# Matmuls of ones between the statistics matmuls ahead of the first loop

## What is computed

```python
xn = _layernorm(x, axis=-1)
# attention: one head of width 512
qkv = einsum('bsc,cf->bsf', xn, Wqkv) + bqkv
q, k, v = qkv.reshape(B, S, 3, 512)[:, :, 0], [:, :, 1], [:, :, 2]
attn = softmax(einsum('bqd,bkd->bqk', q, k) / sqrt(512))
attn_out = einsum('bqd,dc->bqc', einsum('bqk,bkd->bqd', attn, v), Wo) + bo
# 64 experts of rank 8, 16 of them chosen for each token
scores = einsum('bsr,er->bse', einsum('bsd,rd->bsr', xn, Wq_w), keys)
gate = softmax of the 16 largest scores at their places, 0 elsewhere
z = einsum('bsd,nd->bsn', xn, A_w) * gate (8 columns for each expert)
ffn_out = einsum('bsn,on->bso', z, B_w) * 2
out = x + attn_out + ffn_out
```

## Time and profile before

| | before |
|---|---|
| median of 3 runs | 2691.65 us (2690.94 to 2693.8) |
| the profiled execution | 2693.37 us |
| its span | 2691.5 us |
| TensorE matmul busy | 2645.6 us, 98% |
| TensorE weight loads busy | 2166.9 us, 81% |
| VectorE busy | 1884.6 us, 70% |
| ScalarE busy | 980.0 us, 36% |
| GpSimd busy | 346.1 us, 13% |
| DMA | 648.30 MB, mean 241 GB/s |

### The profile page before, as it was taken

One profiled execution on the slowest core, in us unless ns is written; L12 is line 12 of the kernel. 1 busy time (PEld: TensorE's weight loads), 2 busy tenths in 40 slices (PEclk: granted clock), 3 DMA queues, 4 the chain that ended last, 5 costly groups with the idle time before them and its releaser, 6 DMA issues.

```text
span 2691.5 us, 32557 instructions
## 1 busy us (share of the span) xinstructions
PE 2645.6 (98%) x11728; PEld 2166.9 (81%) x11728; DVE 1884.6 (70%) x2423; ACT 980.0 (36%) x1297; POOL 346.1 (13%) x334
## 2 busy tenths in 40 slices
PE   6999999999999999999999999999999999999998
PEld 5777887888878888888888888888888888888787
DVE  7958875567755777676847486684976838668677
ACT  5562335522364234433335332234332333223311
POOL 1011000000000001111103221022220212103140
PEclk9999999999999999999999999999999999999999
DMA  8689856445554457766887758578687775856866
GB/s 321 208 321 343 267 175 196 156 166 183 176 201 139 169 180 242 247 207 233 296 291 290 265 203 301 203 259 314 237 291 273 257 286 204 303 204 244 312 247 222
DMA packets 250915, 648.30 MB, mean 241 GB/s; under 512 B 20864, under 2 KB 45568, under 8 KB 246528
## 3 DMA queue, kind: packets, MB, share of 16 engines
q1 hardware_dynamic: 200528, 471.02, 50.2%
q0 software_dynamic: 30224, 111.16, 11.5%
q10 hardware_dynamic: 20000, 63.99, 6.6%
HBM read 499.27 MB, written 146.83 MB: 240 GB/s over the span
## 4 chain that ended last, share of the span: by engine, by line
PE 82%; DVE 6%; DMA 6%; issue 3%; ACT 3%; SPq 0%; ACTq 0%; DVEq 0%; POOL 0%
PE psum L843 38%; PE psum L2019 13%; PE psum L2021 13%; PE psum L2020 13%; PE psum L773 2%; DMA w_raw<-W_blocks 2%; DMA r_lo<-split_scratch 1%; DMA part_out<-v_scratch 1%; DVE part_out L2430 1%; ACT rows L621 1%; DMA part_out<-x 1%; ACT w_hi L548 1%; DVE r_lo L2303 0%; DVE w_lo L904 0%; DMA xb<-x 0%
## 5 line engine op out<-in xcount | busy, mean ns | idle before, releaser
L904 DVE TENSOR_TENSOR w_lo<-w_raw,w_hi 128x1024 fp32r<-128x1024 f32 x216 | 264.3, 1224 | 353.0 <-ACT w_hi L548 353.0
L548 ACT ACTIVATE w_hi<-w_raw 128x1024 fp32r<-128x1024 f32 x216 | 229.2, 1061 | 676.0 <-PE psum L843 620.8
L843 PE MATMUL psum<-s_hi,w_hi 128*128 128x512 f32 x896 | 352.4, 393 | 8.7 <-DVE rq L1120 3.1
L843 PE MATMUL psum<-w_hi,s_hi 128*128 128x512 f32 x896 | 349.6, 390 | 2.8 <-DVE w_lo L904 2.0
L843 PE MATMUL psum<-s_hi,w_lo 128*128 128x512 f32 x896 | 350.6, 391 | 0.0
L843 PE MATMUL psum<-s_lo,w_hi 128*128 128x512 f32 x896 | 350.6, 391 | 0.0
L843 PE MATMUL psum<-w_hi,s_lo 128*128 128x512 f32 x896 | 348.9, 389 | 0.0
L843 PE MATMUL psum<-w_lo,s_hi 128*128 128x512 f32 x896 | 348.8, 389 | 0.0
L843 PEld LDWEIGHTS psum<-s_hi,w_hi 128*128 128x128 f32 x896 | 169.2, 189 | 48.5 <-issue 8.2
L2019 PE MATMUL psum<-p_hi,r_hi 128*128 128x512 f32 x512 | 203.7, 398 | 3.9 <-DMA r_lo<-split_scratch 2.3
L843 PEld LDWEIGHTS psum<-w_hi,s_hi 128*128 128x128 f32 x896 | 168.2, 188 | 42.0 <-issue 3.8
(11 more groups left out here) (210 smaller groups left out, 4846.6 us busy)
## 6 DMA issues: line engine op xcount, KB each, us to landing
r_hi<-split_scratch SPq DMA_DIRECT2D x208, 512.0 KB, 3.5
r_lo<-split_scratch SPq DMA_DIRECT2D x208, 512.0 KB, 4.6
w_raw<-t_scratch SPq DMA_DIRECT2D x120, 512.0 KB, 4.1
w_raw<-W_blocks SPq DMA_DIRECT2D x104, 512.0 KB, 4.2
split_scratch<-rows POOLq DMA_DIRECT2D x56, 512.0 KB, 4.2
part_out<-x POOLq DMA_DIRECT2D x28, 1024.0 KB, 12.9
out<-part_out SPq DMA_DIRECT2D x28, 1024.0 KB, 8.4
rows<-x ACTq DMA_DIRECT2D x26, 1024.0 KB, 5.5
```

The costliest lines, as they stand in the source:

```text
L548: nc.scalar.activation(w_hi[:, s % RAW], w_tile(g, idx, s), ACT.Copy).then_inc(s_whi, 1)
L843: mm = pe.matmul(psum[:, bank, :], stationary, moving, start=(k == 0 and n == 0 and not chained), stop=(k == HK - 1 and n == 2), skip_grou ...
L904: nc.vector.tensor_tensor(w_lo[:, s % RAW], w_tile(g, idx, s), w_hi[:, s % RAW].bitcast(F32), ALU.subtract).then_inc(s_wlo, 1)
```

## The change

In the tensor program, `idle_matmuls(n)` is new: n matmuls of `ones` by `ones` into the columns 0 to 127 of bank 5, with no wait and no semaphore. It is called with 9 after the mean of tile j = 1 has been spread and ahead of the wait for tile j = 2, with 3 after the last of the four means (the increment of `s_spread` hangs on the matmul before them), and with 6 after the four reciprocal deviations, ahead of the loop. Other engines' programs are as before.

```diff
@@ -872,13 +872,21 @@
                                    part[:, 2, HT + a, j * P:(j + 1) * P], start=True, stop=True)
                 mm.then_inc(s_spread, 1)
 
+        def idle_matmuls(n):
+
+            for _ in range(n):
+                pe.matmul(psum[:, 5, 0:P], ones[:], ones[:], start=True, stop=True)
+
         pe.wait_ge(s_ones, 2)
         for a in range(2):
             for j in range(HT):
+                if a == 0 and j == 2:
+                    idle_matmuls(9)
                 pe.wait_ge(s_diag, HT + 1 if a else j + 1)
                 mm = pe.matmul(psum[:, 6 + a, j * P:(j + 1) * P], ones[:], stat_diag[a][:, j, :],
                                start=True, stop=True)
             mm.then_inc(s_spread, 1)
+            idle_matmuls((3, 6)[a])
         loop(pe, body)
```

## The result

The changed kernel takes 2696.2 us (median of 20 runs, 2692.52 to 2702.26), the kernel before 2691.99 us (20 runs beside it, 2688.04 to 2696.31). The ratio is 1.0014, with a 95% interval of 1.0008 to 1.0020: 4.2 us slower. I had forecast 2691.2 us and a range up to 2694.3.

A forecast was written before the change was run, and what follows sets the result against it. TensorE was taken to bound the kernel, carrying 82% of the chain. Free batches and a faster clock put it 2.9 us ahead, of which 0.5 passes: 2691.65 - 0.5 = 2691.2 us, range 2688.0 to 2694.3.

The forecast's parts named there:

- the cost of the batches: TensorE's head: batches of 9, 3 and 6 take 3.84, 1.28 and 2.56 us within idle time; cost zero, bounds -0.5 to +0.15.
- the clock: First products from 25.09 us: the matmuls of ones bring full pace, 3.2 instead of 6.11 us, TensorE 2.9 us ahead.
- Rival B: Head of TensorE: products of ones don't lift the clock, so nothing changes; 2691.65 us, chance 0.18.
- Rival D: Head batches: matmuls rewriting the same 128 columns don't stream, 0.58 us per record; 2700.0 us, chance 0.03.
- the 0.5 us at the end of the three points: Head: third weight tile, ScalarE's statistics and VectorE are late next, so 0.5 of the 2.9 us gained leaves the head.
- It removes nothing and moves nothing: Whole kernel: the change only adds 18 matmuls, 36 records, with no wait and no semaphore.
- Point 1: Third weight tile in the head: its load takes 13.2 us, so the item starts at 39.1; 1.7 of 2.9 us left.
- C: Later waits: early TensorE makes one idle stretch long enough for the clock to fall, costing 1.6 us; 2692.8 us, chance 0.06.

The follow-up runs named there:

- e3: The changed kernel without the batch of 9; the batches of 3 and 6 stay, 36 instructions more than the kernel before. Ratio 1.0013.
- e12: The changed kernel without the batch of 9, batches of 3 and 6 in three matmuls of up to 512 columns, 12 instructions more than before. Ratio 0.9997.
- e8: The changed kernel with the same columns of ones in 6 matmuls instead of 18, 24 instructions more than the kernel before. Ratio 1.0008.
- e10: The changed kernel without the batch of 9, plus 55 one-column matmuls in the head, 255 instructions more than the kernel before. Ratio 1.0003.
- e11: The changed kernel without the batch of 9, plus 41 one-column matmuls in the head, 199 instructions more than the kernel before. Ratio 0.9995.
- e16: Repeat of e11: batches of 3 and 6 plus one-column matmuls, against the kernel before. Ratio 1.0000.
- e13: The kernel before with 18 one-column matmuls (72 instructions) at the start of phase B alone. Ratio 1.0000.
- e1: The kernel before, unchanged, built and timed a second time. Ratio 0.9997.
- e6: The kernel before with already satisfied waits ahead of the first statistics matmul, 72 instructions more, no matmul of ones. Ratio 1.0011.
- e2: The kernel before with all 18 matmuls of ones ahead of the first statistics matmul, none in the changed kernel's places. Ratio 1.0003.
- e14: The changed kernel with 46 one-column matmuls (184 instructions) more at the start of phase B. Ratio 1.0020.
- e7: The kernel before with already satisfied waits ahead of the first statistics matmul, 36 instructions more, no matmul of ones. Ratio 1.0012.
- e9: The kernel before with 64 one-column matmuls between the head's statistics matmuls, 255 instructions more, no batch of ones. Ratio 1.0004.
- e4: The changed kernel without the batches of 3 and 6; only the batch of 9 stays, 36 instructions more than before. Ratio 1.0011.

## Why the prediction was wrong

**Right: the cost of the batches.** 4.05, 1.49 and 1.55 us of cover used; the burst started at 20.30, 0.18 late where I had 0.15 as a bound, its end and the first product did not move (25.11, before 25.09).

**Right: the clock.** Full pace at 25.1; TensorE would have started the third item at 37.97 (I said 37.9). Rival B is refuted: matmuls of ones lift the clock. In all ten traces with the batches of 3 and 6 the products start at full pace, in all eight without them at the slow one; e3 has only these two batches. Rival D is refuted: 18 records in 4.05 us are 0.21 each.

**Not borne out: the 0.5 us at the end of the three points.** In e12, with the same fast start and the packets nearly in place, the third item starts at 39.03 (I said 39.1) and the step near 64 us comes at 63.92 instead of 64.64, with 0.97 idle (I said 0.5 and 1.2). e3 and e8 are nearly the same (third item 39.03 and 39.30, the step 63.94 and 64.21). That looks like the mechanism. But the other fast starts with no packet in the third tile's load (e10, e11, e16) start the third item at 39.5 to 39.7 and have the step near 64 at 64.81, 64.63 and 65.35, after waits of 1.2 to 1.8 us; their fourth tile lands 0.9 to 1.7 us later than the 10.8 that I used. And e13, whose head is that of the kernel before, has that step at 63.89 with a slow start. This head shows 14, 12 and 9 slow steps in its three traces (before, e1, e13), and with 9 the third item starts at 39.82. So it is shown that TensorE waits for what is late next; the half microsecond is inside what executions of one head differ by. The ratios of e10, e11, e12 and e16 are 1.0003, 0.9995, 0.9997 and 1.0000; none is a gain.

**Wrong: the sentence "It removes nothing and moves nothing".** The failed step is the list of what the change adds. I priced the 18 matmuls by their records on TensorE's timeline and called that all. They are also 72 instructions in a program that is read by DMA in packets of 16 KB, and they move every later packet. I put that term at nothing without a reason. In its place e6, 72 instructions with no matmul added, shows 1.0011 (1.0003 to 1.0020), about 3 us; e2, 71 instructions, shows 1.0003 (0.9994 to 1.0012), and the two intervals overlap. The row was in front of me: the page has a line for the instruction queue, 0.2% of the engines' time, and I passed over it because of the share.

**Wrong with it: a landing taken as fixed.** Point 1 used 13.2 us as the landing of the third tile. It is 14.3 to 14.5 in the three traces of the changed kernel and 14.1 in e14, which has the same phase A; in these a packet comes at 34.0 to 34.4 us, 2.5 to 2.8 ahead of the landing. It is 12.9 to 13.3 in all others, e2 among them, where the packet comes at 34.9, only 0.6 ahead. So instead of 0.5 us early, the traced execution of the changed kernel was 0.8 us late at 64 us. That is a fifth of the 4.2.

**The rivals** held no mechanism of this kind. C had the clock, and the falls at 182 and 244 us are of its kind, but I tied it to the length of the idle stretch (between 2.47 and 3.10 us) and the clock fell after 1.95. My rivals were all about what TensorE does; a case for what the program's length does had no chance at all, and the range ended 1.9 us under the result.

**What stays open.** Shown: 72 and 36 extra instructions that do nothing, at the start, cost about as much as the change (e6, e7); with 12 or 199 at the start, or 72 at the start of phase B, no loss is measured (e12, e11, e16, e13); with 255 (e9, e10) the intervals hold both 1 and a loss of a thousandth. Two loads land later in the traces in which a packet comes 2 us or more ahead of their landing. Not shown is that a packet of 16 KB itself delays a load by 1 to 3 us: no row shows one waiting for the other. Not settled either is how the 4 us divide. In the traced execution the idle time at 2010 us is 2.4 us more than before (2.91, 0.53), with some seven slow steps behind it (1.4 us), and the head is 0.8 us late; but e14 keeps a loss without that idle time, and the traced executions differ by several us in phase A whether their kernel loses or not. So the failed step is known, and the way from 72 instructions to 4.2 us is in part argued.

## What to carry to other kernels

An instruction added to TensorE's program moved the fetches of all of it that came behind. In a kernel that is bound to within a few us by loads, a change that is hidden on its engine can be worth less than what it shifts by its mere length; add instructions that do nothing, in the same number, as a control before believing a difference of a thousandth. The warm-up put TensorE 2.8 us ahead at the third item (37.97 against 40.79), and no run shows a gain in time from it, because TensorE then waited for the third tile and for VectorE: look for what is late next before buying clock. And take more than one trace of a kernel before reading a difference of 1 us out of it; three traces of one head differed by 0.75 us at 64 us.

## What the runs showed of the hardware

- TensorE's program comes on the page's queue q8 in packets of 16 KB, about one in 28 to 33 us of products (42.8, 71.4 and 99.5 us; 1980 and 2013 us, kernel before). 36 more instructions gave a stall of 2.0 to 2.2 us by "issue" when the loop turned back (e3, e4, e7); with 0, 12, 24, 71, 72, 199 and 255 what "issue" released there was 0.53 us or less.
- Matmuls of ones by ones in F32 lift TensorE's clock: with the batches of 3 and 6 alone the slow steps at 25 us were gone (e3); with the batch of 9 alone, which ends 8 us before the first product, they were not (e4).
- The product near 2010 us came 3.1 us after the seventh load of v had landed, in all thirteen traces in which TensorE waited there. That load took 12.3 to 15.7 us with no instruction packet in it and 16.1 to 18.3 with one 2 us or more ahead of its landing.
- The clock fell after an idle stretch of 1.95 us (changed kernel, 182 us) and stayed up after one of 2.47. The length of an idle stretch alone doesn't tell.
